# Sixteen-batch attention and expert block: batch 0's maxima by a small product, other identity products, a new order

## What is computed

```
x = x + layernorm(attention(layernorm(x)))      # 16 heads of 8 features, scale 1/sqrt(128), then w_out
x = x + layernorm(ffn(layernorm(x)))            # 8 experts (top 2, softmax weights) and a shared expert
attention: softmax(q @ k.T / sqrt(c)) @ v       # per head
ffn: sum over e of rw[t, e] * (silu(x Wg[e]) * (x Wu[e])) @ Wd[e]  +  (silu(x Sg) * (x Su)) @ Sd
```

## Time and profile before

| what | us |
|---|---|
| median of 3 runs | 373.18 (371.95 to 376.94) |
| the profiled execution, its whole time | 371.26 |
| its span, first to last instruction | 369.5 |
| PE, DVE, ACT, POOL busy in the span | 350.6, 313.2, 267.3, 200.5 |

### The profile page before, as it was taken

How to read it: one execution, slowest core, us unless ns; L and a number is a source line. 1 busy time by engine, 2 the same in 40 slices (tenths; PEclk the granted TensorE clock), 3 DMA queues, 4 the chain that set the end, 5 groups by cost and what they waited for, 6 DMA issues and landing times.

```text
span 369.5 us, 10052 instructions
## 1 busy us (share of the span) xinstructions
PE 350.6 (95%) x3304; PEld 227.0 (61%) x3304; DVE 313.2 (85%) x788; ACT 267.3 (72%) x511; POOL 200.5 (54%) x518
## 2 busy tenths in 40 slices
PE   8998999999999989999999999999999999998892
PEld 7856555544665546575757475666765556667772
DVE  8796698989999996999897899999999986768661
ACT  4752688699788876969886797788768868864522
POOL 7333053324663544777565465755763576767654
PEclk9999999999999999999999999999999999999998
DMA  2266988554665574266456455487265041322211
GB/s 84 67 148 139 208 168 179 142 116 128 163 178 104 153 152 139 75 132 163 132 170 166 128 117 149 129 187 166 81 185 142 19 130 33 116 64 71 56 34 31
DMA packets 59922, 45.65 MB, mean 124 GB/s; under 512 B 8966, under 2 KB 56966, under 8 KB 59870
## 3 DMA queue, kind: packets, MB, share of 16 engines
q1 hardware_dynamic: 59870, 45.00, 48.5%
HBM read 26.69 MB, written 17.81 MB: 120 GB/s over the span
## 4 chain that ended last, share of the span: by engine, by line
PE 60%; issue 10%; POOL 10%; DVE 9%; ACT 4%; DMA 3%; SPq 2%; POOLq 0%; DVEq 0%; ACTq 0%
PE pvp L661 12%; PE bank_d L831 8%; PE bank_d L815 8%; PE sc L645 8%; PE sc L629 6%; PE bank_d L816 5%; DVE mx L1010 4%; PE bank_a L714 3%; POOL rstd L1152 2%; POOL hidden L1219 2%; PE bank_d L668 2%; DMA ks<-qk_dram 2%; POOL parts L1163 2%; DVE rden L1042 1%; PE bank_d L806 1%
## 5 line engine op out<-in xcount | busy, mean ns | idle before, releaser
L1010 DVE TENSOR_REDUCE mx<-sc 128x4 f32<-128x1024 f32 x128 | 154.2, 1217 | 18.5 <-PE sc L629 17.7
L859 ACT ACTIVATE pr<-sc 128x1024 f32<-128x1024 f32 x128 | 130.7, 1024 | 27.2 <-PE sc L645 26.4
L661 PE MATMUL pvp<-pr,va 128*32 128x256 f32 x1024 | 68.5, 385 | 0.0
L815 PE MATMUL bank_d<-x3T,wg_sb 128*128 128x256 f32 x160 | 54.3, 421 | 2.4 <-DVE hidden L1108 2.0
L645 PE MATMUL sc<-qs,ks 51*128 51x256 bf16 x512 | 49.6, 274 | 1.8 <-DMA qs<-mT 0.9
L629 PE MATMUL sc<-ks,qs 48*128 48x256 bf16 x512 | 49.6, 272 | 1.8 <-DVE mx L1010 1.1
L1219 POOL TENSOR_TENSOR hidden<-hidden,rwb 128x256 f32<-128x256 f32 x60 | 42.3, 729 | 12.6 <-DMA rwb<-rw_dram 11.8
L816 PE MATMUL bank_d<-x3T,wu_sb 128*128 128x256 f32 x160 | 47.6, 379 | 0.0
L1152 POOL TENSOR_TENSOR rstd<-vareps,mhalf 128x2 f32<-128x2 f32 x64 | 44.5, 696 | 0.0
L661 PEld LDWEIGHTS pvp<-pr,va 128*32 128x32 f32 x1024 | 26.7, 109 | 25.1 <-issue 12.4
L831 PE MATMUL bank_d<-wd_sb,hidden 128*128 128x128 f32 x320 | 39.4, 278 | 2.2 <-POOL hidden L1219 2.2
(11 more groups left out here) (115 smaller groups left out, 506.8 us busy)
## 6 DMA issues: line engine op xcount, KB each, us to landing
rwb<-rw_dram SPq DMA_DIRECT2D x30, 256.0 KB, 4.2
qk_dram<-parts SPq DMA_DIRECT2D x30, 192.0 KB, 2.7
qs<-qk_dram SPq DMA_DIRECT2D x30, 192.0 KB, 4.1
ks<-qk_dram SPq DMA_DIRECT2D x30, 192.0 KB, 4.9
qk_dram<-parts SPq DMA_DIRECT2D x30, 128.0 KB, 2.6
pv_dram<-pv_sb SPq DMA_DIRECT2D x14, 256.0 KB, 2.2
x_sb<-in_L_attn_x_dram SPq DMA_DIRECT2D x16, 128.0 KB, 2.7
out_dram<-x SPq DMA_DIRECT2D x16, 128.0 KB, 1.8
```

Source lines behind the costliest of these rows:

```text
L661: mm = pe.matmul(pvp[32 * j:32 * j + 32, g, :], values[:, X * c + 4 * g + j, 32 * tt:32 * tt + 32], pr[:, k, c * N:(c + 1) * N], start=(tt ...
L815: pe.matmul(bank_d[bank][:, 0:N], wg_sb[:, ORDER[n], :], x3T[b % 2][:], start=True, stop=True)
L859: nc.scalar.activation(pr[:, 2 * s:2 * s + 2, :].rearrange("p k n -> p (k n)"), sc[PAIR["s2", b, s]][:].rearrange("p u c n -> p (u c n)"), ...
L1010: nc.vector.tensor_reduce(mx[b % 2][:, :, :, s].rearrange("p c u -> p u c"), sc[PAIR["s1", b, s]][:], AX.X, ALU.max).then_inc(max_done, 1)
```

## The change

1. **Batch 0's maxima.** Its `s2` no longer has rows 48 to 50. Instead a second product per head and tile adds the negative maxima into the same PSUM result: the stationary operand is a column of a new tile `msel`, broadcast to 128, that is -1 in the three rows of step s; the moving one is mT of batch 0, now held as 24 rows at partition 0 and 24 at 64. `maxT` of batch 0 is four products in place of two, `max_copy` two copies in place of one. The DMA `max_stack` of batch 0 is gone, and `load_minus` is waited for by batch 1. `msel` is made on POOL, a memset and six selects one after another.
2. **Identity products.** FILL has 75 in place of 56, FILL_SCORES 2 in place of 19. Ahead of `xT` of batch 0 there are 17 in both.
3. **The order.** TIMES is written anew for nearly every step. The first steps of each engine are listed below; from batch 2 on the moves are mostly of a few places. `load_wgu` (7 DMAs) and `load_wd` (3) change places: the first now comes at tick 39, the second at 111.

```diff
 def s2(b, s):
     if s == 0:
-        pe.wait_ge(max_stacked[b % 2], landed(2, b))
         if b == 0:
+            pe.wait_ge(max_copied, 2)
+            pe.wait_ge(msel_done, 6)
+        else:
+            pe.wait_ge(max_stacked[b % 2], landed1(2, b))
+        if b == 1:
             pe.wait_ge(minus_load, DMA * 2)
     for c in range(TT):
         for u in range(2):
-            rows = slice(64 * u, 64 * u + ROWS_MAX)
-            mm = pe.matmul(sc[pair][:, u, c, :], k[rows, s, c * P:(c + 1) * P], q[rows, s, :], start=True, stop=True)
+            rows = slice(64 * u, 64 * u + (ROWS_MAX if b else ROWS))
+            mm = pe.matmul(sc[pair][:, u, c, :], k[rows, s, c * P:(c + 1) * P], q[rows, s, :], start=True, stop=b > 0)
+        if b == 0:
+            for u in range(2):
+                rows = slice(64 * u, 64 * u + 3 * X)
+                mm = pe.matmul(sc[pair][:, u, c, :], msel[rows, s:s + 1].broadcast_to([3 * X, P]), mT[0][rows], start=False, stop=True)
...
-                if (b := due(tick, "max_stack")) is not None:
-                    sp.wait_ge(max_copied, b + 1)
+                if (b := due(tick, "max_stack")) is not None and b:
+                    sp.wait_ge(max_copied, b + 2)
...
+                if due(tick, "msel") is not None:
+                    nc.gpsimd.memset(msel[:], 0.0).then_inc(msel_zeroed, 1)
+                    pool.wait_ge(msel_zeroed, 1)
+                    for n in range(6):
+                        first = 64 * (n // 3) + X * (n % 3)
+                        nc.gpsimd.affine_select(out=msel[:], in_=msel[:], compare_op=ALU.not_equal, fill=-1.0, base=-first,
+                                                pattern=[[-1, X]], channel_multiplier=1).then_inc(msel_done, 1)
+                        pool.wait_ge(msel_done, n + 1)
...
 FILL = {
-    "maxT": {0: 9, 2: 1}, "qk": {0: 2}, "s1_2": {0: 1, 1: 1}, "s1_3": {1: 1}, "s1_6": {2: 3, 3: 2}, "s2_3": {1: 4},
-    "s2_4": {0: 3}, "s2_5": {0: 4}, "sel1": {0: 3}, "xT": {0: 17, 3: 4, 5: 1},
+    "maxT": {0: 8}, "qk": {0: 3, 3: 1}, "s1_0": {0: 2}, "s1_1": {1: 1}, "s1_2": {1: 3}, "s1_3": {1: 3, 2: 1},
+    "s1_4": {0: 3, 1: 1}, "s1_6": {0: 3, 1: 2}, "s1_7": {2: 1}, "s2_0": {0: 3}, "s2_1": {0: 1}, "s2_2": {0: 1, 1: 2},
+    "s2_3": {1: 2}, "s2_4": {0: 2}, "s2_5": {1: 1}, "s2_7": {1: 1}, "sel1": {0: 4}, "v": {2: 1},
+    "xT": {0: 17, 2: 1, 3: 3, 5: 1, 6: 3},
 }
```

More of the change, by code:

```diff
@@ L35 @@
 TIMES = {
[L36 to L43, removed]
-    "pickm": [23],
-    "apply1": [24, 41, 52, 88, 95, 181, 197, 202, 337, 459, 489, 664, 890, 982, 1109, 1241],
@@ L46 @@
[L46 to L61, removed]
+    "load_x": [0, 12, 13, 14, 53, 108, 143, 181, 196, 209, 280, 397, 443, 517, 643, 808],
+    "stats1": [15, 28, 34, 37, 104, 126, 203, 216, 232, 352, 433, 567, 654, 793, 929, 1010],
@@ new lines @@
+    "lay1": [17],
+    "load_wout": [18],
+    "aggr1": [19, 32, 36, 75, 124, 153, 211, 252, 345, 378, 472, 600, 748, 861, 977, 1100],
+    "lay0b": [20],
+    "rstd1": [21, 35, 41, 77, 128, 155, 241, 262, 347, 414, 497, 673, 790, 904, 1027, 1198],
+    "lay0a": [22],
+    "pickm": [23],
+    "apply1": [24, 43, 47, 84, 134, 167, 250, 307, 419, 426, 629, 779, 862, 981, 1091, 1217],
+    "minusm": [25],
+    "wqk": [26],
+    "xT": [27, 52, 66, 97, 140, 188, 267, 360, 466, 625, 741, 858, 974, 1087, 1205, 1328],
@@ L172 @@
-    "down": [451, 659, 789, 883, 1005, 1119, 1237, 1367, 1453, 1563, 1643, 1720, 1790, 1844, 1893, 1903],
-    "down_copy": [463, 678, 800, 895, 1028, 1134, 1248, 1380, 1464, 1572, 1656, 1734, 1802, 1853, 1898, 1906],
[5 rows of a table removed]
-    "store": [520, 757, 886, 972, 1132, 1216, 1375, 1443, 1591, 1657, 1695, 1796, 1864, 1885, 1913, 1915],
+    "ql_copy": [57],
+    "kl_copy": [58],
+    "s1_0": [60, 114, 163, 224, 281, 388, 503, 603, 694, 837, 934, 1065, 1169, 1286, 1400, 1496],
+    "kh_copy": [61],
+    "s1_1": [63, 120, 168, 234, 305, 407, 522, 614, 721, 850, 951, 1085, 1197, 1303, 1414, 1521],
@@ new lines @@
+    "max_0": [64, 117, 166, 226, 285, 393, 507, 608, 701, 840, 940, 1069, 1174, 1290, 1408, 1500],
+    "selq": [67],
+    "max_1": [70, 121, 170, 237, 308, 413, 526, 620, 724, 856, 960, 1088, 1204, 1307, 1418, 1524],
+    "s1_2": [71, 127, 176, 244, 312, 416, 528, 628, 731, 860, 970, 1099, 1213, 1315, 1428, 1542],
+    "qh_copy": [72],
+    "spill": [None, 73, 100, 132, 187, 284, 336, 470, 593, 690, 786, 973, 1052, 1209, 1283, 1407],
[4 rows of a table added]
+    "msel": [82],
[3 rows of a table added]
+    "stack": [None, 90, 125, 159, 201, 325, 421, 492, 632, 752, 866, 1003, 1122, 1237, 1321, 1444],
[4 rows of a table added]
@@ new lines @@
+    "msplit": [105, 162, 233, 286, 385, 491, 607, 719, 835, 926, 1057, 1168, 1289, 1391, 1491, 1623],
+    "maxT": [107, 169, 261, 306, 396, 500, 613, 728, 846, 953, 1072, 1186, 1306, 1423, 1506, 1635],
+    "max_copy": [109, 172, 264, 313, 406, 504, 616, 733, 849, 959, 1076, 1191, 1309, 1427, 1510, 1639],
+    "load_wd": [111],
+    "s2_0": [112, 194, 287, 342, 434, 541, 651, 766, 880, 1002, 1102, 1247, 1337, 1457, 1544, 1659],
+    "exp_0": [115, 198, 289, 344, 438, 545, 655, 770, 888, 1006, 1105, 1251, 1340, 1461, 1549, 1662],
@@ new lines @@
+    "load_minus": [118],
[16 rows of a table added]
+    "max_stack": [None, 173, 266, 317, 412, 509, 622, 739, 855, 962, 1080, 1196, 1310, 1432, 1514, 1641],
+    "exp_7": [175, 245, 335, 409, 524, 623, 735, 853, 971, 1086, 1199, 1317, 1429, 1537, 1629, 1747],
+    "pv_3": [180, 253, 343, 425, 532, 631, 743, 865, 984, 1093, 1216, 1325, 1462, 1546, 1655, 1767],
+    "pv_copy": [186, 258, 357, 431, 538, 659, 757, 886, 992, 1101, 1221, 1343, 1466, 1561, 1669, 1775],
+    "osel": [192, None, None, None, None, None, None, None, None, None, None, None, None, None, None, 1779],
@@ L189 @@
 FILL = {
-    "maxT": {0: 9, 2: 1}, "qk": {0: 2}, "s1_2": {0: 1, 1: 1}, "s1_3": {1: 1}, "s1_6": {2: 3, 3: 2}, "s2_3": {1: 4},
-    "s2_4": {0: 3}, "s2_5": {0: 4}, "sel1": {0: 3}, "xT": {0: 17, 3: 4, 5: 1},
+    "maxT": {0: 8},
+    "qk": {0: 3, 3: 1},
+    "s1_0": {0: 2},
+    "s1_1": {1: 1},
+    "s1_2": {1: 3},
+    "s1_3": {1: 3, 2: 1},
+    "s1_4": {0: 3, 1: 1},
+    "s1_6": {0: 3, 1: 2},
+    "s1_7": {2: 1},
+    "s2_0": {0: 3},
+    "s2_1": {0: 1},
+    "s2_2": {0: 1, 1: 2},
+    "s2_3": {1: 2},
+    "s2_4": {0: 2},
+    "s2_5": {1: 1},
+    "s2_7": {1: 1},
+    "sel1": {0: 4},
+    "v": {2: 1},
+    "xT": {0: 17, 2: 1, 3: 3, 5: 1, 6: 3},
 }
 FILL_SCORES = {
-    ("s1", 0, 2): 1,
-    ("s1", 0, 3): 1,
-    ("s1", 1, 0): 5,
-    ("s1", 1, 3): 1,
-    ("s1", 1, 4): 2,
-    ("s1", 2, 7): 1,
-    ("s1", 3, 6): 1,
-    ("s2", 0, 0): 2,
-    ("s2", 0, 4): 2,
-    ("s2", 0, 5): 1,
-    ("s2", 1, 3): 2,
+    ("s2", 2, 0): 1,
+    ("s2", 3, 3): 1,
 }
@@ L296, in sandwich @@
         mrest = ring(2, "mrest", [P, TT, 2, X])
-        mT = ring(2, "mT", [3 * H, N], BF16)
+        mT = ring(2, "mT", [64 + 3 * X, N], BF16)
+        msel = sb("msel", [64 + 3 * X, X], BF16)
         pr = sb("pr", [P, H, TT * N])
@@ L682, in _ @@
                     for c in range(TT):
-                        mm = pe.matmul(bank_a[0:3 * H, c * P:(c + 1) * P], mp[b % 2][:, c].rearrange("p u a x -> p (u a x)"),
-                                       ident_bf[:], start=True, stop=True)
+                        if b:
+                            mm = pe.matmul(bank_a[0:3 * H, c * P:(c + 1) * P], mp[b % 2][:, c].rearrange("p u a x -> p (u a x)"),
+                                           ident_bf[:], start=True, stop=True)
+                        else:
+                            for u in range(2):
+                                mm = pe.matmul(bank_a[64 * u:64 * u + 3 * X, c * P:(c + 1) * P],
+                                               mp[b % 2][:, c, u].rearrange("p a x -> p (a x)"), ident_bf[:], start=True, stop=True)
                     mm.then_inc(maxT_done, 1)
-                    a_empty = (max_copied, b + 1)
+                    a_empty = (max_copied, b + 2)
                 for s in range(X):
@@ L863, in _ @@
                     act.wait_ge(maxT_done, b + 1)
-                    if b >= 2:
-                        act.wait_ge(max_stacked[b % 2], landed(2, b - 2))
-                    nc.scalar.copy(mT[b % 2][:], bank_a[0:3 * H, 0:N]).then_inc(max_copied, 1)
+                    if b == 2:
+                        act.wait_ge(s2_done, X)
+                    if b >= 3:
+                        act.wait_ge(max_stacked[b % 2], landed1(2, b - 2))
+                    if b:
+                        nc.scalar.copy(mT[b % 2][0:3 * H], bank_a[0:3 * H, 0:N]).then_inc(max_copied, 1)
+                    else:
+                        for u in range(2):
+                            rows = slice(64 * u, 64 * u + 3 * X)
+                            nc.scalar.copy(mT[0][rows], bank_a[rows, 0:N]).then_inc(max_copied, 1)
                 if (b := due(tick, "apply1")) is not None:
```

72 lines of the change are left out of this document (32 added, 40 removed), and 150 rows, old and new, of the table TIMES.

## The result

The changed kernel is slower: 378.22 us median (375.35 to 380.12, 19 runs) against 372.03 us (370.02 to 376.94, 19 runs) on the same chip, ratio 1.0155, 95% interval 1.0136 to 1.0175, some 5.8 us by that ratio. The forecast was 371.3 us, with a range of 366.5 to 376.5. The profiled execution took 377.63 us, span 375.8.

A forecast was written before the change was run, and what follows sets the result against it. PE was taken to set the pace from about 60 us, and to wait for others at the beginning. Gains of 0.4 + 1.5 = 1.9 us gave 369.4 profiled, 371.3 us as median; eight-in-ten range 366.5 to 376.5 us.

The forecast's parts named there:

- the small products: Batch 0's `s2` steps: eight products in place of four add 0.3 us to each of eight steps, pairs overlapping.
- Rival (b): Doubled `s2` steps hold two PSUM buffers, batch 1's maxima wait: 2.6 us lost, 375.8 us if no hole closes; chance 0.20.
- my walk: Step-by-step timing of batch 0's and 1's scores: `max_7.1` ends at 44.8 us, `exp_7.0` at 49.0; 0.4 us ahead taken.
- one more behind: After `max_7.1`, one exponential more is already done, so `max_1.2` starts at 47.0 in place of 48.07 us.
- at nothing where the wait remains: After batch 0's maxima, 31 identity products replace about 37: worth nothing where PE still waits, at most 1.3 us otherwise.
- they can buy no speed there: Identity products after batch 0's maxima: granted clock is 1.00 in every window, so they cannot raise it.
- The first maximum: Batch 0's first maximum on DVE starts at about 17.25 in place of 17.82 us, 0.6 us earlier.
- `s2_0.0` with the copies: Batch 0's first `s2` waits only for the mT copies and runs at about 29.7 in place of 35.79 us.
- Stack 1: Batch 1's stack from DRAM, which its first scores await, lands at 31.4 in place of 31.1 us.
- The copy order: `kl_copy` ahead of `kh_copy`, `ql_copy` last: first scores start at 16.1 instead of 17.4 us.
- The hole at `down.1`: PE's 2.15 us idle at batch 1's `down` closes as its weights come earlier; gain taken at 1.5 us.
- the rest of the order: Hundreds of other moves, shifts of a few places: counted as zero, with 3 us to either side.

## Why the prediction was wrong, by its own steps

**The failed term: the small products.** The sum had 0.3 us for each of eight steps. The rows say 0.86 - 0.31 = 0.55 us, 4.4 us over eight in place of 2.4. Two of the reasons were mine to see. The price was taken from four products of 48 and 51 rows, and carried over to an alternation of 48 and 24 rows, which no row of before shows; there I should have kept both ends. And an upper end was in hand, the serial price that the prediction quotes from the Trainium skill ("TensorE: Matmul & The Clock Gate", section "Wait — 56ns, not 53.3ns?"): 109 ns for each product, 0.44 us for the four added; I set it aside as disproved by the earlier trace rows. Even it was 0.1 us too low, since the four that were there grew slower too. With 0.25 us more for each of the six steps ahead of `s1_7.1` my walk gives 46.3 us for the end of `max_7.1`, and 47.1 with the identity products below; it ended at 47.3 us in place of 44.8.

**Rival (b) happened.** Its sign was there: `max_7.1` later than 46 us, DVE idle for PE. Its price of 2.6 us was too low for the same reason, and so was its chance of 0.20: the walk showed DVE waiting ahead of most maxima of batch 1, and a stretch that hangs on PE's `s2` steps takes each addition in full. I had let the exponential "one more behind" pay it back.

**Identity products "at nothing where the wait remains".** Not where the wait was gone: 34.32 to 35.19 us stand between a finished maximum (34.38) and `s1_2.1`. Locally this is shown, some 0.4 us at each of two places. For the end no kernel showed a gain from thinning them in this order, except the one without small products (0.9986 against 1.0109), where the hole at 215 us and the slow stretch behind it were gone too. And the step "they can buy no speed there", read from a clock of 1.00 with the identity products in place, was wrong: without them the clock fell in each of the four kernels, in before's order too.

**What held.** The first maximum at 17.29 us (17.25 said), partly by luck: the first selection was 0.34 us later than said, and the stretch from the copies to that maximum 0.3 us shorter. `s2_0.0` with the copies, though at 30.67 in place of 29.7: eight identity products stood ahead of `maxT.0` until 29.49, 0.6 us after its input was ready, which I hadn't counted, and the two copies of mT ran one behind the other (29.82 to 30.57 us) and not overlapped. Stack 1 at 31.35 us (31.4). Batch 1's first maximum at 31.96 (31.85). The copy order. The hole at `down.1`: closed, as said. But its 1.5 us of gain was counted against a kernel that is on time, and the changed one was 3 us late there; the late kernel used the hole up, as the trace of before's order with the small product shows (+4.6 us ahead of it, +2.4 behind). Gain and loss were not two terms to be added.

**The second failed term: the rest of the order.** I counted it as zero with 3 us to either side. In sum that came out: the small product at 24 rows cost 1.0155 in the new order and 1.0165 in the old, at 48 rows 1.0086 and 1.0062, differences within the intervals. But it is a sum of two large parts, and that they nearly cancel is luck. The same PE work, from batch 6's `down` to the end of the span, takes 131.0 us before and 134.6 us in the changed kernel, and PE is busy in it for as long:

```profile
238.49:369.50 131.01, 121.27 (x1095) 82.95 (x1094) 100.57 (x309) 88.56 (x177) 80.43 (x208) 0.99 0.36 94
241.24:375.80 134.56, 121.01 (x1096) 82.91 (x1094) 99.90 (x311) 87.32 (x175) 79.33 (x203) 0.98 0.37 91
235.64:370.00 134.36, 121.00 (x1096) 82.92 (x1094) 99.39 (x311) 87.31 (x175) 79.33 (x203) 0.99 0.36 91
```

These are before, the changed kernel and the changed kernel with 48 rows. PE idles 9.7 to 11.2 us of this part in all six kernels with before's later order, and 11.7 to 15.4 us in all eight with the new one. The three waits between 240 and 300 us shown above are most of the difference in the changed kernel: a hole opened at batch 8's `down`, of the kind that I had named for the 3 us. Ahead of that part the new order gains: with 48 rows it reaches batch 6's `down` at 235.64 us, 2.9 us earlier than before, and has lost all of it at the end. Of the changed kernel's 6.4 us, by the profiled executions, 2.8 are there at 241 us and 3.6 come behind.

**The sum again.** 5.8 us slower: of it 0.7 to 1.0%, 2.6 to 3.8 us, is the change between row counts (shown, by the 48-row kernels in both orders; 8 times 0.32 us in the traces is 2.5). The other 0.6 to 0.9% is what stays with 48 rows. In before's order it is the small product even when it is cheap: 8 times 0.22 us, 1.8 us, is seen by 50 us, and that 2.3 us stay at the end isn't explained. In the new order it isn't shown to be the small product's, since the order without any stands at 1.0109; there the 3.4 us lost behind batch 6's `down` are as large as the rest. The base was off too: the forecast started from a median of three runs, 373.18 us, and nineteen gave 372.03, so on the same base it would have been 1.2 us lower. Not explained either is why the profiled executions of some kernels are 1.5 to 5 us faster than their medians; the microseconds read from traces are therefore those of single executions. Doing the four score products first and then the four small ones, which would change the row count once a step, was not tried. No kernel here beats the one before; even with the small products and the identity products left out, the new order only equals it.

## What to carry to other kernels

When products are added between others on PE, compare their row counts: 24 rows between 48-row products cost 0.21 us a pair, zero-padded to 48 they cost 0.11. Price an added operation by a row that has the same alternation, and where no row has it, keep the serial price as the upper end and ask whether the engine is waited for in just that stretch. And a gain in a later hole is not to be added to a loss ahead of it: the hole swallows the loss, and the gain is gone. A new order whose sum is near zero may still hold a gain and a loss worth separating: time the same work, from one product to the end, in both traces.
